# Graph layer on one core: gathered rows stored as high and low halves, three rounded products in place of an fp32 one, one-hots scaled on ScalarE, and packed edge fields

## What is computed

```python
xn = layernorm(x)
gathered = edge_weight[:, None] * xn[src]
agg = segment_sum(gathered, dst, 6250) + node_vec1
x = x + agg + linear_attention(xn)       # 4 heads, one 64x64 key-value sum per head
x = x + moe(layernorm(x))                # 8 experts, top 2 of each node
```

## Time and the profile before

| what | value |
|---|---|
| median of 3 runs | 2327.5 us |
| the profiled execution, its own time | 2324.71 us |
| span of its trace | 2322.8 us |
| TensorE busy | 2139.4 us, 92% |
| VectorE busy | 2041.2 us, 88% |
| GpSimd busy | 1638.6 us, 71% |
| ScalarE busy | 1215.4 us, 52% |

### The profile page before, as it was taken

How to read it: one execution, slowest core, us unless ns; L and a number is a source line. 1 busy time by engine, 2 the same in 40 slices (tenths; PEclk the granted TensorE clock), 3 DMA queues, 4 the chain that set the end, 5 groups by cost and what they waited for, 6 DMA issues and landing times. The chain is left out here.

```text
span 2322.8 us, 45681 instructions
## 1 busy us (share of the span) xinstructions
PE 2139.4 (92%) x16549; PEld 1879.9 (81%) x16550; DVE 2041.2 (88%) x3324; ACT 1215.4 (52%) x1688; POOL 1638.6 (71%) x1364
## 2 busy tenths in 40 slices
PE   7997799999999999999999999999999449999993
PEld 4665678888888888888888888888899449898892
DVE  7988999999999999999999999999788677666662
ACT  2336755555555555555555555554232257666561
POOL 3770067777777777777777777777777338888873
PEclk9997999999999999999999999999999679999997
DMA  4542433333333333333333333233555634544455
GB/s 139 158 114 73 127 114 92 89 90 101 92 91 100 88 92 92 101 89 89 92 101 92 91 99 91 90 90 91 141 152 155 199 60 74 76 76 75 75 74 137
DMA packets 160928, 235.85 MB, mean 102 GB/s; under 512 B 54834, under 2 KB 121805, under 8 KB 160490
## 3 DMA queue, kind: packets, MB, share of 16 engines
q0 software_dynamic: 70896, 164.43, 28.4%
q1 hardware_dynamic: 75536, 55.29, 8.6%
q10 hardware_dynamic: 14314, 13.68, 1.7%
HBM read 186.46 MB, written 53.24 MB: 103 GB/s over the span
## 5 line engine op out<-in xcount | busy, mean ns | idle before, releaser
L810 POOL DMA_INDIRECT picked<-xn_dram,place x1029 | 1185.8, 1152 | 445.7 <-issue 299.5
L908 PE MATMUL bank<-picked,pick_w 128*128 128x256 f32 x2058 | 501.4, 380 | 2.7 <-DMA picked<-xn_dram,place 2.7
L1020 ACT COPY stage<-bank 128x512 f32<-128x512 f32 x343 | 201.3, 587 | 496.5 <-PE bank L896 485.1
L908 PEld LDWEIGHTS bank<-picked,pick_w 128*128 128x128 f32 x2058 | 391.5, 190 | 56.4 <-DVE pick_w L1269 3.0
L974 ACT COPY field_rep<-fields 128x1666 bf16<-128x1666 bf16 (+1 forms) x235 | 398.4, 1718 | 0.8 <-DVE vals L1151 0.8
L904 PE MATMUL bank<-window,stage 128*128 128x256 f32 x1568 | 381.4, 386 | 0.0
L1262 DVE TENSOR_TENSOR hot_w<-hots,cur 128x1536 bf16<-128x1536 bf16 x343 | 328.5, 958 | 11.9
L904 PEld LDWEIGHTS bank<-window,stage 128*128 128x128 f32 x1568 | 282.6, 190 | 30.5 <-ACT stage L1020 0.2
L1258 DVE TENSOR_TENSOR hots<-iota_j,cur 128x1408 bf16<-128x1408 bf16 x343 | 302.6, 882 | 0.0
L896 PE MATMUL bank<-hot_w,hots 128*128 128x128 bf16 x4116 | 285.4, 219 | 1.5 <-DVE hot_w L1262 1.4
L904 PE MATMUL bank<-stage 128*128 128x256 f32 x1176 | 286.0, 386 | 0.0
(11 more groups left out here) (247 smaller groups left out, 3388.1 us busy)
## 6 DMA issues: line engine op xcount, KB each, us to landing
picked<-xn_dram,place POOLq DMA_INDIRECT x1029
xn_dram<-xn ACTq DMA_DIRECT2D x49, 128.0 KB, 1.9
xT_dram<-xT ACTq DMA_DIRECT2D x49, 128.0 KB, 2.2
base_dram<-acc SPq DMA_DIRECT2D x7, 896.0 KB
sum_dram<-acc SPq DMA_DIRECT2D x7, 896.0 KB
z_dram<-vals SPq DMA_DIRECT2D x7, 896.0 KB, 9.0
out_dram<-sum_dram SPq DMA_DIRECT2D x1, 6250.0 KB, 22.4
acc<-in_x_dram SPq DMA_DIRECT2D x6, 896.0 KB, 6.8
```

What stands on the lines that cost most here:

```text
L810: pool.indirect_dma_start(out=picked[:, i % SETS * PICK + q, :], out_offset=None, in_=xn_dram, in_offset=bass.IndirectOffsetOnAxis(ap=plac ...
L908: mm = pe.matmul(sum_ps[pp], pick_w[i % SETS][:, q, :], picked[:, i % SETS * PICK + q, :], start=False, stop=(q == PICK - 1))
L1020: act.copy(block_sb[pp].rearrange("p j c -> p (j c)"), banks[pp][:, :]).then_inc(a_copied, 1)
```

## The change

1. The front also stores each row as a high half rounded to fp32r (ScalarE copies it) and a low half, the rest (VectorE subtracts it), side by side in `xh_dram`: 2048 bytes a row where `xn_dram` has 1024. The store is issued by ScalarE.
2. The gathers read `xh_dram`. Three matmuls in fp32r take the place of each fp32 one: high one-hot by high rows, high by low, and low by high.
3. The scaled one-hots of the picked edges, `pick_h` and `pick_l`, are made by ScalarE: six activations of 128x128 a pass with the weight of each partition as their scale, where VectorE made `pick_w` in one product. `cur_w` goes.
4. Source row and destination row travel as one packed 16-bit field (`END`), so FIELDS is 4 for 5. VectorE takes them apart again in the table (`part`, `make_list`). The one-hots are compared with bit patterns that stand in the new tile `ends`.
5. Buffers are kept in SETS = 3 sets for 4. A gather waits for the pass three before it.

```diff
-FIELDS = 5
+FIELDS = 4
@@ front, ScalarE and VectorE @@
+                act.copy(xh[t % DEPTH][:, 0, :], xn[t % DEPTH][:, :]).then_inc(high_done, 1)
...
+            def store_parts(t):
+                act.wait_ge(low_done, t + 1)
+                act.dma_start(xh_dram[t * P:(t + 1) * P, :], xh[t % DEPTH][:, :, :].rearrange("p k d -> p (k d)").bitcast(F32)).then_inc(stored[t % DEPTH], 16)
...
-                act.copy(fields[:, DST, at, :], dst_r[:, :, :]).then_inc(placed, 1)
-                act.copy(fields[:, SRC, at, :], src_r[:, :, :]).then_inc(placed, 1)
...
+            def low_part(t):
+                dve.wait_ge(high_done, t + 1)
+                dve.tensor_tensor(xh[t % DEPTH][:, 1, :], xn[t % DEPTH][:, :], xh[t % DEPTH][:, 0, :].bitcast(F32), ALU.subtract).then_inc(low_done, 1)
...
+                    dve.scalar_tensor_tensor(out=fields[:, END, at, :].bitcast(U16), in0=dst_r[:, :, :], scalar=float(LOWEST * P), in1=src_r[:, :, :],
+                                             op0=ALU.add, op1=ALU.add).then_inc(kept, 1)
@@ edge sum, GpSimd @@
-                used = t - SETS if i >= SETS else t - BU + SETS if i < BU - SETS else t - BU
-                if used >= 0:
-                    pool.wait_ge(o_done, used + 3)
+                if t >= SETS:
+                    pool.wait_ge(o_done, t - SETS + 3)
                 for q in range(PICK):
-                    pool.indirect_dma_start(out=picked[:, i % SETS * PICK + q, :], out_offset=None, in_=xn_dram,
+                    pool.indirect_dma_start(out=picked_f[:, t % SETS * PICK + q, :], out_offset=None, in_=xh_dram,
@@ edge sum, TensorE @@
-                    mm = pe.matmul(sum_ps[pp], pick_w[i % SETS][:, q, :], picked[:, i % SETS * PICK + q, :], start=False, stop=(q == PICK - 1))
+                    high, low = (picked[:, t % SETS * PICK + q, m * D:(m + 1) * D] for m in range(2))
+                    pe.matmul(sum_ps[pp], pick_h[t % SETS][:, q, :], high, start=False, stop=False)
+                    pe.matmul(sum_ps[pp], pick_h[t % SETS][:, q, :], low, start=False, stop=False)
+                    mm = pe.matmul(sum_ps[pp], pick_l[t % 2][:, q, :], high, start=False, stop=(q == PICK - 1))
@@ edge sum, ScalarE @@
+            def picks(t):
+                g, b = divmod(t, NT)
+                act.wait_ge(hot_done, t + 1)
+                if t >= 2:
+                    act.wait_ge(o_done, t + 1)
+                for to, of in ((pick_h[t % SETS], weight_h[g % 2][:, :, :].bitcast(F32)), (pick_l[t % 2], weight_l[g % 2])):
+                    for q in range(PICK):
+                        ins = act.activation(to[:, q, :], hot[t % SETS][:, q, :], ACT.Copy, scale=of[:, b, q:q + 1])
+                ins.then_inc(pick_done, 1)
...
                         evacuate(t + i + 1, (odd + i + 1) % 2)
+                        picks(t + i + 1)
@@ edge sum, VectorE @@
+            def part(s, j, par):
+                dve.wait_ge(unpacked, s + 1)
+                bits = table[par][:, :, :].bitcast(U16)
+                both, dst = (bits[:, :, at:at + DENSE][:, :, bass.ds(j, 1)].rearrange("p b a -> p (a b)") for at in (AT_SRC, PICK))
+                dve.tensor_scalar(dst, both, 0x7F80, None, ALU.bitwise_and)
+                dve.tensor_scalar(both, both, P - 1, 0x3F80, ALU.bitwise_and, ALU.bitwise_or).then_inc(parted, 1)
...
-            def picks(t, i, odd):
-                dve.wait_ge(hot_done, t + 1)
-                dve.tensor_tensor(pick_w[i % SETS][:, :, :].rearrange("p q (b r) -> p q b r", r=REP),
```

More of the change, by code:

```diff
@@ L26 @@
 I32 = mybir.dt.int32
+U16 = mybir.dt.uint16
 BF16 = mybir.dt.bfloat16
@@ L215, in front @@
         xn = [sb(f"xn{i}", [P, D]) for i in range(DEPTH)]
+        xh = [sb(f"xh{i}", [P, 2, D], F32R) for i in range(DEPTH)]
         xT = [sb(f"xT{i}", [P, 2, P]) for i in range(DEPTH)]
@@ L383, in _ @@
                     repeat_sample(t)
-                for k in range(NC):
-                    if t - APART[k] == 4:
-                        places(k)
+            store_parts(LAST)
         @block.tensor
@@ L606, in _ @@
                 shift(t)
+            for t in range(DEPTH - 1):
+                low_part(t)
             for t in range(NT):
@@ L895, in blocks, with rows @@
                     for part in range(3):
-                        mm = pe.matmul(block_ps(pp, j), hot[buf][:, PICK + DENSE + j, :], hot_w[buf][:, part, j, :],
+                        mm = pe.matmul(block_ps(pp, j), hot[buf][:, PICK + j, :], hot_w[buf][:, part, j, :],
                                        start=(part == 0), stop=(part == 2))
                 mm.then_inc(a_done, 1)
-            def rows(t, i, u, pp, par):
+            def rows(t, pp, par):
                 pe.wait_ge(a_copied, t + 3)
@@ L1248, in sort, with hots @@
                 slots(s)
-                if s % 2 == 0 and s > 0:
+                if s % 2 == 1:
+                    part(s - 1, (s - 1) // 2, 0)
+                elif s > 0:
                     make_list(s - 1, s // 2 - 1, s // 2 - 1, 0)
-            def hots(t, i, odd, free):
-                if free is not None:
-                    dve.wait_ge(a_done, free)
+            def hots(t, i, odd):
+                if t >= SETS:
+                    dve.wait_ge(a_done, t)
+                    dve.wait_ge(pick_done, t - SETS + 1)
@@ L1319, in unit @@
                     if more and i == 1:
+                        if odd == par:
+                            part(s - 1, q, 1 - par)
                         in_row(s)
```

184 lines of the change are left out of this document (101 added, 83 removed).

## The result

The changed kernel took 2366.5 us (median of 4 runs, 2362.3 to 2371.7) against 2325.3 for the kernel before on the same chip (2320.8 to 2329.2): a ratio of 1.018, 95% interval 1.016 to 1.020. It is slower by 41 us. I had forecast 2336, and a range of 2272 to 2395. The time lies in the range and the sign is the forecast one, but the likeliest time is 30 us too low: I had forecast a change of +11 us, and it is nearly four times that.

What follows compares the result with a forecast made beforehand. It took TensorE as the bound with GpSimd half a microsecond under it, and GpSimd's gathers as the bound after. Edge sum +8, last group -7, front +12, early sort -2 gave +11, so 2336 us, range 2272 to 2395.

Steps and rivals of the forecast that it cites:

- the last group: Last group of the edge sum: 49 passes at 0.15 us less, -7 us.
- The share f of the chance sum: Edge-sum unit: part of the by-chance hold of gathers that really occurs; taken as 0.7, giving a unit of 31.2 us.
- Rival 1: Edge sum: holds go and TensorE sets the pace, 28.5 us a unit, about 2220 us in all; chance 0.15.
- Rival 3: Edge sum: wide-row gathers dearer (0.1 us each makes 2439 us) or ScalarE the bound (+20 us); chance 0.10.
- Rival 2: Edge sum: full chance collisions of gathers with VectorE products, 33.0 us a unit, +82 us, about 2410; chance 0.15.
- my own case: Edge sum: GpSimd bounds with a hold of 0.16 to 0.27 us, units of 30.1 to 32.2, 2285 to 2380; chance 0.60.
- The front: Front: VectorE's added subtraction puts 0.2 to 0.25 us a tile on the path, 49 x 0.23, +12 us (bounds 3 and 20).
- the early sort's -2: Early sort: eight `vals` less save 8 us; `part`, longer lists and set-up for `ends` give back 6; -2 us.
- The unit of before: Edge sum: old unit taken as 31.05 us, so the new 31.2 was 0.18 more, 42 units, +8 us.

Runs made afterwards that it cites:

- with two gathers: Changed kernel with two gathers a pass instead of three, the third operand reusing the second's rows; 2244.8 us, 0.965 of before.
- the pieces: Changed kernel with VectorE's long products cut into 2 to 4 pieces; 2273.5 us, 0.978 of before; on the other sort of chip 2506.1 and 2487.5.
- the narrow rows: Changed kernel with gathers of 1024-byte rows instead of 2048, the low product reusing the high rows; 2364.2 us, 1.016 of before; again 2360.6, 1.014.
- the front's part alone: Kernel before with only the front's high copy, low subtraction and store of both parts added, which nothing reads; 2360.3 us, 1.015 of before.
- four buffers: Changed kernel with four instead of three front buffers for `xn` and `xh`; 2434.6 us, 0.958 of before, on the other sort of chip.

## Where the prediction was right, and where it failed

**Which engine bounds, right.** GpSimd's gathers were to take over from TensorE, with TensorE idle for picked rows and 21 gathers filling the unit. They did. The unit came out at 31.28 for 31.2, the mean gather at 1.186 for 1.19. VectorE is busy 26.43 us of that unit for 27.4. The share f of the chance sum is (1.186 - 0.945) x 31.28/10.8 = 0.70, the value taken; before it had been 0.52. I had reasoned to it only by nearness to the last group, so a part of that match is luck.

**TensorE, right.** The high and low matmuls are 0.12 apart, the table's 34 take 2.91 from start to start for 2.92, and with gathers out of the way a unit is 28.5.

**ScalarE, right where it counts.** Three scaled one-hots take 0.99 us, 0.30 each and not 0.27; ScalarE is busy 27.34 for 27.4. TensorE waited for `pick_l` only 8.2 us in 1180, and with two gathers TensorE was full at 28.5. The Trainium skill's figures (ScalarE: Activation LUTs, "What ACT_TABLE_LOAD costs") made an estimate of 0.29, and the trace agrees.

**Rivals.** Rival 1, TensorE as the bound at 28.5, needed a mean hold below 0.11: it stood at 0.241. With the pieces it fell to 0.118, and the unit to 28.9. Rival 3 is out: its dear wide rows by the narrow rows, its dear activations by the 0.30. Rival 2, full chance, would have been 33.0 a unit, a mean hold of (33.0 - 26.15)/21 = 0.33. The sign that I gave it, a hold past 0.24, could tell nothing, as it lies inside my own case of 0.16 to 0.27; the 0.241 stands right on it.

**The last group, right**: -6.2 for -7.

**The front, wrong.** The step that failed is "0.2 to 0.25 goes on the path: 49 x 0.23, +12 us (bounds 3 and 20)", with the new store "inside the bound of 20". The stretch that the term is part of grew by 26 us in the profiled run and by some 35 in the mean; with the front's part alone it grew by 42 in the profile and the kernel by 36. The price of the subtraction was right (0.419 for 0.412). Missing was a wait. The change makes the normalization wait for two stores a tile instead of one, and the second can only be issued when the subtraction is done, a tile later, so three buffers no longer cover it: some 16 us. I had priced the store by the DMA engines' busy share (60%, and 74% after) and not by its latency against the buffers' age, and had not walked `stored` through the three buffers, though the diff shows its count go from 16 to 32. The subtraction itself may have been sized about right: taking it off VectorE gave back 7 or 14 us beside four buffers, for the 12 of the term. The last 8 or so were not parted; ScalarE's copy and its issue of the store, which I had priced at nothing, are the work that is left. Nor was the early sort's -2 parted from this term.

**The unit of before, wrong by 0.3.** I took 31.05, the length of one window, for the unit and called its growth 0.18; but a window is as long as its reader makes it, and it measures no period. Two gathers 147 apart, seven units, say 215.3/7 = 30.76, and my own sum of TensorE's parts had been 30.8. Against that, 31.28 is +0.52, 42 times, 22 us where I had 8. (By 30.76, GpSimd's 21 gathers and gaps, 30.6, were within 0.15 us of the bound, not half a microsecond under it.) The unit after was right, the unit before was not.

These two, 16 and 15 us, with the +0.8 of the last group and -2.7 behind the edge sum, are the 29 between the forecast +11 and the measured +40 of the profiled runs. The step that failed in the first is the overlap: a store that my sum priced at nothing, and for which the next `xn` had to wait.

## What to carry to other kernels

When a change speeds up the engine that bounds a loop, look for the second bound before pricing the gain: here it lay less than half a microsecond under the first, and it was made of gaps and holds that no busy share shows. Measure a loop's period between two like instructions many turns apart, never from one window. And where a change adds a store to a ring of buffers, walk the ring: when is the buffer wanted again, when is the last store issued, and when does it land. A gather that is held by the other engine's long products is let in sooner if these are cut in pieces, worth 4% on the first sort of chip, even though the pieces are more work; on the other sort they gained nothing.

## What the runs showed of the hardware

- An indirect gather of 128 rows takes 0.945 us and 0.30 of gap, with rows of 1 or 2 KB alike; if it begins while VectorE multiplies or compares two SBUF operands, it ends 0.81 to 0.82 us behind that product (472 of 511 such gathers of the changed kernel; the other 39 began at the same moment as the product and were free). Shorter products halved the mean hold, from 0.241 to 0.118 us.
- Chips, or batches, differ. On two of the five chips of the experiments the kernel before took 2325 us, on three 2545 to 2549, with TensorE standing by issue for up to 1.5 us at a time in and behind its chains of small matmuls. The change was 1.8% slower on the one sort and 3 to 4% faster on the other, so a single chip's verdict did not carry over. An estimate for the first sort: pieces, four front buffers and the subtraction on GpSimd together would take some 2245 us, the 2273.5 of the pieces less the 28 by which the first gather comes sooner (303.5 for 332.1). That version ran only on the other sort, where it wasn't the fastest.
